# Row sums from a column of ones, two output banks, and one ring of four PSUM banks for every other product

## The reference

```python
# layer 0, attention (8 heads of 64) and top-2 of 8 experts
kv  = concat(layernorm(ctx), layernorm(x) * kv_gate)
sim = (q * 64**-0.5) @ k.T - max;  sim = where(valid, sim, -1e30)
x  += tanh(g) * (softmax(sim) @ v) @ Wout
act = silu(x @ w1.T) * (x @ w3.T);  x += tanh(g) * sum_of_two_experts(act @ w2.T)
# layer 1, attention (16 heads of 64) and a quantised feed-forward with a conv over tokens
x  += tanh(g) * (softmax(q @ k.T / 8 + mask) @ v) @ Wout
h   = silu(conv3(bit_linear(layernorm(x), w1)));  x += tanh(g) * bit_linear(h, w2)
```

## Time and profile before

| | |
|---|---|
| runs | 1537.44, 1544.24, 1548.83 us |
| span of the profiled execution | 1538.1 us, 45142 instructions |
| PE busy | 1278.3 us (83%) |
| POOL busy | 1107.9 us (72%) |
| DVE busy | 1053.8 us (69%) |
| ACT busy | 979.1 us (64%) |
| DMA queues, share of 16 engines | 55.7% on q1, 10.6% on q10 |

### The profile page before, as it was taken

One profiled execution on the slowest core, in us unless ns is written; L12 is line 12 of the kernel. 1 busy time (PEld: TensorE's weight loads), 2 busy tenths in 40 slices (PEclk: granted clock), 3 DMA queues, 4 the chain that ended last, 5 costly groups with the idle time before them and its releaser, 6 DMA issues.

```text
span 1538.1 us, 45142 instructions
## 1 busy us (share of the span) xinstructions
PE 1278.3 (83%) x16918; PEld 994.2 (65%) x16918; DVE 1053.8 (69%) x2830; ACT 979.1 (64%) x2319; POOL 1107.9 (72%) x1359
## 2 busy tenths in 40 slices
PE   0778787679878989878999999899999999998852
PEld 0556565557667866656887887667676676766642
DVE  4768788977556656665666666777777777877634
ACT  2778787456455666554656566678777777777631
POOL 4768788687557755466777776788878888787653
PEclk9989999879999989989999999999999999999965
DMA  9599997486999954368999997344555444555310
GB/s 314 134 193 235 246 239 174 83 221 188 218 233 252 233 95 97 73 159 171 247 258 231 269 247 181 79 97 98 105 91 94 90 105 94 106 82 91 79 32 6
DMA packets 438329, 239.96 MB, mean 156 GB/s; under 512 B 388848, under 2 KB 420320, under 8 KB 429024
## 3 DMA queue, kind: packets, MB, share of 16 engines
q1 hardware_dynamic: 408216, 178.51, 55.7%
q10 hardware_dynamic: 26824, 51.22, 10.6%
q0 software_dynamic: 3072, 7.34, 1.6%
HBM read 107.78 MB, written 35.50 MB: 93 GB/s over the span
## 4 chain that ended last, share of the span: by engine, by line
PE 39%; ACT 13%; DVE 12%; POOL 11%; issue 9%; DMA 9%; DVEq 3%; SPq 2%; ACTq 1%; POOLq 0%
PE bank_ring L1088 9%; PE bank_ring L1126 6%; PE bank_ring L1074 5%; PE bank_out L1107 5%; DVE scores L1340 4%; DMA expert_up<-experts_up 4%; ACT scores L849 4%; PE bank_x L1187 3%; POOL probs L654 3%; PE bank_scores L1048 3%; ACT probs L856 3%; PE bank_x L1140 3%; DMA probs_turned<-probs 3%; ACT values L876 2%; DMA context<-in_ctx 2%
## 5 line engine op out<-in xcount | busy, mean ns | idle before, releaser
L654 POOL TENSOR_TENSOR probs<-scores,probs 112x487 f16<-112x487 f32 x384 | 425.0, 1123 | 234.2 <-ACT probs L856 229.1
L849 ACT ACTIVATE scores<-scores,score_min 112x487 f32<-112x487 f32 x384 | 265.8, 693 | 121.0 <-DVE score_min L1340 118.2
L1357 DVE SCALAR_TENSOR_TENSOR values<-bank_ring,values 128x512 f16<-128x512 f32 x192 | 132.4, 689 | 216.4 <-ACT values L876 216.3
L1340 DVE CUSTOM_DVE_ANT_0 scores<-bank_scores,mask 112x487 f32<-112x487 f32 x384 | 238.1, 657 | 2.9 <-PE bank_scores L1048 2.9
L856 ACT ACTIVATE probs<-scores 112x487 f16<-112x487 f32 x384 | 214.2, 604 | 24.4 <-DMA probs_turned<-probs 9.0
L1088 PE MATMUL bank_ring<-weights,kv_B 128*128 128x128 f16 x3072 | 198.3, 223 | 1.2 <-DVE keys L1352 1.2
L876 ACT ACTIVATE values<-bank_ring 128x512 f16<-128x512 f32 x192 | 112.9, 588 | 128.9 <-PE bank_out L1107 125.2
L1088 PEld LDWEIGHTS bank_ring<-weights,kv_B 128*128 128x128 f16 x3072 | 187.2, 100 | 10.5 <-DVE keys L1352 2.0
L1107 PE MATMUL bank_out<-values,probs_turned 128*128 128x64 f16 x4608 | 171.9, 195 | 17.7 <-issue 11.4
L1074 PE MATMUL bank_ring<-kv_B,weights 128*128 128x488 f16 x768 | 181.0, 372 | 0.0
L1107 PEld LDWEIGHTS bank_out<-values,probs_turned 128*128 128x128 f16 x4608 | 160.1, 100 | 21.4 <-issue 14.0
(11 more groups left out here) (230 smaller groups left out, 2470.9 us busy)
## 6 DMA issues: line engine op xcount, KB each, us to landing
expert_up<-experts_up SPq DMA_DIRECT2D x43, 1024.0 KB, 5.5
expert_down<-experts_down SPq DMA_DIRECT2D x43, 512.0 KB, 6.6
raw_weights<-in_weights ACTq DMA_DIRECT2D x8, 1536.0 KB, 10.7
experts_up<-expert_up ACTq DMA_DIRECT2D x8, 1024.0 KB, 4.4
raw_weights<-in_weights ACTq DMA_DIRECT2D x6, 1024.0 KB, 8.0
probs_turned<-probs SPq DMA_TRANSPOSE x384
context_turned_B<-kv_B ACTq DMA_DIRECT2D x16, 375.0 KB, 8.7
kv_B<-context_turned_B ACTq DMA_DIRECT2D x16, 375.0 KB, 3.7
```

What stands on the lines that cost most here:

```text
L654: pool.tensor_tensor(PR[:, u % 4, 1, 0:KEYS], S[:, u % 4, 0:KEYS], PR[:, u % 4, 0, 0:KEYS], ALU.subtract).then_inc(probs_split, 1)
L849: act_e.activation(S[:, u % 4, 0:KEYS], S[:, u % 4, 0:KEYS], ACT.Exp, bias=rmin[:, u % 4:u % 4 + 1], scale=-1.0, accum_out=rsum[:, g % 2, ...
L1340: dve.tensor_tensor_reduce(out=S[:, u % 4, 0:KEYS], in0=bS[u % 2][0:TOK, 0:KEYS], in1=mask[:, m, 0:KEYS], scale=1.0, scalar=3.0e38, op0=AL ...
L1357: dve.scalar_tensor_tensor(vN[:, j % 2, 1].rearrange("p t d -> p (t d)"), bank("v", j)[:], 1 / WSCALE, vN[:, j % 2, 0].rearrange("p t d -> ...
```

## The change

It does four things.

1. The values get a 65th column per head (`vN` is laid out as 8 blocks of 66 columns): ones in the hi half, zeros in the lo half. So `sum_values` writes the row sum beside the 64 output columns, and the exponentials on ACT no longer accumulate it.
2. There are two output banks. `norm_out` runs twice per group, for four heads each, in step 4g+4 and in step 4g+6 (for two groups 4g+5), and now stands ahead of the reads of `late(j-1)` in DVE's order. `sum_values` waits for the half that was two halves back.
3. ACT rounds the probabilities of both heads in one instruction of 974 elements instead of two of 487.
4. `bank_x0` and `bank_x1` are gone. Queries, `down` and all side products take their place in a common ring of four banks, in PE's order. A product waits until the one four places before it has been read. Two waits that the single bank had implied are now written out (`o_proj` on `o_turn`, `f_up` on `f_turn`).

PE's own order of products stays as it was.

The diff, cut to its core:

```diff
-X0_TASKS = ("m_gate", "route", "wsum")
...
+def side_tasks():
+    tasks = []
     for j in range(FIRST_STEP, LAST_STEP + 1):
...
+        tasks += early(j) + late(j)
+    return tasks
+SIDE_AT = {t: i + 1 for i, t in enumerate(side_tasks())}
...
-RING = 3
+RING = 4
 def ring_uses():
     uses = []
     for j in range(FIRST_STEP, LAST_STEP + 1):
         m = micro(j)
         if is_pair(j + 2):
-            uses.append(("k", j + 2))
+            uses += [("q", j + 2), ("k", j + 2)]
         if m[0]:
             uses.append(m[0])
+        uses += early(j)
         if is_pair(j):
             uses.append(("v", j))
+        if m[1]:
+            uses.append(m[1])
+        uses += late(j)
         if m[2]:
             uses.append(m[2])
...
-        vN = sb("values", [128, 2, 2, 4, 128], F16)
+        vN = sb("values", [128, 2, 2, 8, HW], F16)
...
-        bO, bX0, bX1 = ps("bank_out"), ps("bank_x0"), ps("bank_x1")
+        bO = [ps("bank_out_0"), ps("bank_out_1")]
...
             def split_probs(u):
-                pool.wait_ge(probs_ready, u + 1)
+                pool.wait_ge(probs_ready, u // 2 + 1)
...
             def exp(u):
-                g = u // 8
                 act_e.wait_ge(scores_masked, u + 1)
-                if u % 8 == 0 and g >= 2:
-                    act_e.wait_ge(out_normed, g - 1)
                 act_e.activation(S[:, u % 4, 0:KEYS], S[:, u % 4, 0:KEYS], ACT.Exp,
-                                 bias=rmin[:, u % 4:u % 4 + 1], scale=-1.0,
-                                 accum_out=rsum[:, g % 2, u % 8:u % 8 + 1])
+                                 bias=rmin[:, u % 4:u % 4 + 1], scale=-1.0)
-            def round_probs(u):
+            def round_probs(j):
+                u = 2 * j
                 if u >= 4:
                     act_e.wait_ge(turned[(u - 4) % PT_BUFS], turns_done(u - 4))
+                    act_e.wait_ge(turned[(u - 3) % PT_BUFS], turns_done(u - 3))
-                act_e.activation(PR[:, u % 4, 0, 0:KEYS], S[:, u % 4, 0:KEYS], ACT.Copy).then_inc(probs_ready, 1)
+                act_e.activation(PR[:, u % 4:u % 4 + 2, 0, 0:KEYS], S[:, u % 4:u % 4 + 2, 0:KEYS], ACT.Copy)\
+                    .then_inc(probs_ready, 1)
...
                 last = RING_USES[i]
-                if last[0] == "k":
+                if last[0] == "q":
+                    pe.wait_ge(q_split, last[1] + 1)
+                elif last[0] == "k":
                     pe.wait_ge(k_split, last[1] + 1)
                 elif last[0] == "v":
                     pe.wait_ge(v_split, last[1] + 1)
+                elif last[0] == "up":
+                    pe.wait_ge(gated, 2 * tile(last[1], last[2]) + last[3] + 1)
+                elif last[0] == "down":
+                    pe.wait_ge(down_copied, tile(last[1], last[2]) + 1)
                 else:
-                    pe.wait_ge(gated, 2 * tile(last[1], last[2]) + last[3] + 1)
+                    pe.wait_ge(side_drained, SIDE_AT[last])
...
             def sum_values(j):
                 pe.wait_ge(v_split, j + 1)
+                m = j // 2
+                if j % 2 == 0 and m >= 2:
+                    pe.wait_ge(out_normed, m - 1)
                 for h in range(2):
                     u = 2 * j + h
-                    if u % 8 == 0:
-                        pe.wait_ge(out_normed, u // 8)
...
-                            last = pe.matmul(bO[:, col:col + HD], PT[u % PT_BUFS][:, at:at + 128],
-                                             vN[:, j % 2, b, t, HD * h:HD * h + HD], start=i == 0, stop=i == 11)
+                            last = pe.matmul(bO[m % 2][:, col:col + HD + 1], PT[u % PT_BUFS][:, at:at + 128],
+                                             vN[:, j % 2, b, 2 * t + h, 0:HD + 1], start=i == 0, stop=i == 11)
...
             def down(b, i):
                 t = tile(b, i)
-                pe.wait_ge(x0_drained, X0_AT[("down", b, i)] - 1)
+                ring_free("down", b, i)
+                bD = bank("down", b, i)
...
             def part(task):
                 name, n = task[0], task[1]
-                if name in X0_TASKS:
-                    pe.wait_ge(x0_drained, X0_AT[task] - 1)
-                else:
-                    pe.wait_ge(x1_drained, X1_AT[task] - 1)
+                ring_free(*task)
+                bX = bank(*task)
...
+            for i in range(2):
+                dve.memset(vN[:, i, 0, :, HD:HD + 1], 1.0)
+                dve.memset(vN[:, i, 1, :, HD:HD + 1], 0.0)
...
-            def norm_out(g):
-                dve.wait_ge(values_summed, 8 * g + 8)
-                if g:
-                    dve.wait_ge(x1_filled, X1_AT[("o_turn", g - 1)])
-                dve.reciprocal(rinv[:], rsum[:, g % 2])
+            def norm_out(m):
+                g, half = m // 2, m % 2
+                dve.wait_ge(values_summed, 4 * m + 4)
+                if g and half == 0:
+                    dve.wait_ge(side_filled, SIDE_AT[("o_turn", g - 1)])
+                heads = bO[half][0:TOK, 0:4 * HW].rearrange("p (h d) -> p h d", h=4)
+                r = rinv[:, 4 * half:4 * half + 4].rearrange("p (h o) -> p h o", o=1)
+                dve.reciprocal(r, heads[:, :, HD:HD + 1])
                 dve.drain()
...
+                dve.tensor_tensor(wide[:, 256 * half:256 * half + 256].rearrange("p (h d) -> p h d", h=4),
+                                  heads[:, :, 0:HD], r.to_broadcast([TOK, 4, HD]), ALU.mult).then_inc(out_normed, 1)
...
+                for g in range(PAIRS // 4):
+                    if j == 4 * g + 4:
+                        norm_out(2 * g)
+                    if slack(g) and j == 4 * g + 6:
+                        norm_out(2 * g + 1)
                 for t in late(j - 1):
                     part(t)
-                for g in range(PAIRS // 4):
-                    if slack(g) and j == 4 * g + 6:
-                        norm_out(g)
...
                     if not slack(g) and j == 4 * g + 5:
-                        norm_out(g)
+                        norm_out(2 * g + 1)
```

More of the change, by code:

```diff
@@ L21 @@
 HD = 64
+HW = HD + 2
 EXPERTS, EB = 8, 4
@@ L207, in l1_chunk @@
     return range(j - L1_STEP, j - L1_STEP + 1) if 0 <= j - L1_STEP < L1_CHUNKS else range(0)
-X0_TASKS = ("m_gate", "route", "wsum")
-def ordinals():
-    x0, x1 = [], []
+def side_tasks():
+    tasks = []
     for j in range(FIRST_STEP, LAST_STEP + 1):
-        if is_pair(j + 2):
-            x0.append(("q", j + 2))
-        for t in early(j):
-            (x0 if t[0] in X0_TASKS else x1).append(t)
-        found = micro(j)
-        x0 += [m[:3] for m in found[:2] if m and m[0] == "down"]
-        for t in late(j):
-            (x0 if t[0] in X0_TASKS else x1).append(t)
-    return {t: i + 1 for i, t in enumerate(x0)}, {t: i + 1 for i, t in enumerate(x1)}
-X0_AT, X1_AT = ordinals()
+        tasks += early(j) + late(j)
+    return tasks
+SIDE_AT = {t: i + 1 for i, t in enumerate(side_tasks())}
 def halves_in_step(j):
     return is_pair(j)
-RING = 3
+RING = 4
 def ring_uses():
@@ L509, in load_expert @@
                     if t >= 2:
-                        sp.wait_ge(x0_filled, X0_AT[("down",) + ((b, i - 2) if i >= 2 else (0, TILES[0] - 2 + i))])
+                        sp.wait_ge(down_ready, t - 1)
                     sp.dma_start(edown[:, t % 2], down_dram[e]).then_inc(down_loaded[t % 2], 16)
@@ L514, in store_result @@
                 t = tile(b, i)
-                sp.wait_ge(x0_drained, X0_AT[("down", b, i)])
+                sp.wait_ge(down_copied, t + 1)
                 sp.dma_start(ys[b][128 * i:128 * i + 128, :], yo[:, t % 2]).then_inc(y_stored[t % 2], 16)
@@ L661, in split_hidden @@
                 if t >= 2:
-                    pool.wait_ge(x0_filled, X0_AT[("down",) + ((b, i - 2) if i >= 2 else (0, TILES[0] - 2 + i))])
+                    pool.wait_ge(down_ready, t - 1)
                 pool.wait_ge(gated, h + 1)
@@ L875, in round_v @@
                     act_e.wait_ge(values_summed, 2 * (j - 1))
-                act_e.activation(vN[:, j % 2, 0], bank("v", j)[:].rearrange("p (t d) -> p t d", t=4), ACT.Copy,
+                act_e.activation(vN[:, j % 2, 0, :, 0:HD], bank("v", j)[:].rearrange("p (t d) -> p t d", t=8), ACT.Copy,
                                  scale=1 / WSCALE).then_inc(v_hi, 1)
@@ L888, in copy_result @@
                 t = tile(b, i)
-                act_e.wait_ge(x0_filled, X0_AT[("down", b, i)])
+                act_e.wait_ge(down_ready, t + 1)
                 if t >= 2:
                     act_e.wait_ge(y_stored[t % 2], 16 * (t // 2))
-                act_e.activation(yo[:, t % 2], bX0[:, 0:DIM], ACT.Copy).then_inc(x0_drained, 1)
+                act_e.activation(yo[:, t % 2], bank("down", b, i)[:, 0:DIM], ACT.Copy).then_inc(down_copied, 1)
             def part(task):
@@ L1055, in proj_q @@
                 wq, _, _, step = layer_chunks(j)
-                pe.wait_ge(x0_drained, X0_AT[("q", j)] - 1)
+                ring_free("q", j)
+                bQ = bank("q", j)
                 i = 0
@@ L1060, in proj_q @@
```

(11 more changed lines are left out.)

178 lines of the change are left out of this document (88 added, 90 removed).

## The result

The changed kernel took 1575.33, 1577.46, 1599.03 and 1575.47 us, median 1576.47 of all four; the kernel before 1537.44 to 1549.43 us, median 1546.53 over four runs. The ratio is 1.020, 95% interval 1.016 to 1.024; it leaves out the disturbed 1599.03. The forecast was 1573, range 1541 to 1598, and slower with 0.63. The profiled execution has a span of 1573.6 us, 35.5 more than before.

A forecast was written before the change was run, and what follows sets the result against it. PE was taken as nearly full in both expert stretches, so new waits lengthen the kernel. Terms -5 + 30 - 5 + 27 - 20 - 6 + 6 + 2 = +29 on 1538.1 give 1567, plus 6.1 for the runs: 1573 us, range 1541 to 1598.

The forecast's parts named there:

- The ring in the expert steps: Steps 39 to 55 and 80 to 103: new PE stalls for banks not yet read, 37.6 and 25.0 us.
- The half normalisations' 4.9: Expert stretches: a half normalisation ahead of a late read costs 0.7 us, seven times in either stretch, 4.9 us each.
- What the loads of weights hide: Steps 39 to 55: a later PE waits less for experts' weights, hiding an estimated 8 us of stalls.
- The first rival: Steps 39 to 55: the experts' loads set the pace and stalls only fill waits; 1547 us, chance 0.17.
- The gain in steps 104 to 183: Steps 104 to 183: bank waits of 3.5 us per eight steps go, about 1.5 come new; -20 us.
- Steps 0 to 38: First stretch: removed bank waits mostly turn into the next wait, behind POOL's mask and the router; -5 us.
- The clock: PE: ten new stalls over 2 us, about half followed by the lower clock level; +6 us.
- The third rival: PE: each stall of over 0.8 us, about 39, lowers the clock; 1617 us, chance 0.06.
- The column of ones: PE's sums: 24 more columns for each of 192 pairs at 0.42 ns a column; +2 us.
- The fourth rival: PE's sums: the odd width of 65 columns costs as much as 128; 1640 us, chance 0.02.
- The read-outs on ACT: ACT: 384 row-sum read-outs of 0.19 us disappear, 73 us of busy time; costed at nothing in kernel time.
- The second rival: Softmax on ACT is the path, so shorter exponentials let DVE's key reads come earlier; 1530 us, chance 0.13.

The follow-up runs named there:

- ring of five, keys first: Ring of four banks made five, with one output bank and DVE's keys' lo half moved ahead of the gating; 1514.91 us, ratio 0.982 against the kernel before.
- the ring of four alone: Changed kernel with parts 1 to 3 undone, leaving only the common ring of four banks; 1568.99 us, ratio 1.014 against the kernel before.
- the keys first: Changed kernel with DVE's lo half of the keys moved ahead of the gating and early reads; 1552.10 us, ratio 1.001 against the kernel before.

## Why the prediction was right, and where its terms were off

The mechanism was right: the two expert stretches and the waits in them came as forecast. That the whole span is off by only 6.5 us is in part luck. Steps 0 to 38 and 104 to 183 came out 12 us each above their terms, against 7 in steps 39 to 55 below theirs and the 8 us for clock and column that stood beside the table.

- *The ring in the expert steps, the largest term: right.* The stalls stand where the subtraction of starts and read ends put them, at `down`, the values and the first expert half. 37.6 + 4.9 us were counted in steps 39 to 55 and 38.5 measured; 29.9 and 29.0 in steps 80 to 103. The half normalisations' 4.9 in the first stretch was 3.6, and went into waits for weights. The ring alone has the loss, and either another distance or another order of DVE's reads takes it away.
- *What the loads of weights hide: mis-sized.* I read the 23.0 us of waits for weights as all in steps 39 to 55, and those of 80 to 103 as none; 19.9 stood in the first and 3.1 in the second. I took 8 us; 17.5 of 19.9 went (19.9 to 2.4). 38.5 - 17.5, less the 4.0 of other waits at `down` that the trace of before has there, plus 5.8 more busy us of PE, is 22.8; the stretch grew by 22.6. The first rival had this mechanism, but the stalls outgrew the waits that could hide them. It falls as the whole story: the stretch did not keep its 189 us, and the DMA share fell from 0.96 to 0.82.
- *The gain in steps 104 to 183: the step that failed.* -20 was forecast, -7.6 came. I costed the single rounding at nothing, covered by the sums two steps later. The path is another: through ACT's order to the values' hi half and from there to a bank of the ring; undoing it gave 5.9 us, of which that wait shows 3.1. The waits on single banks went as forecast (all 40.4 us of PE's waits there before are gone), but the new ones came to 27.2 us where I had about 15: 15.4 in place of 11 for values behind late reads, 11.1 in place of 3 behind the keys. PE's busy time is 5.8 us longer, where I had 2 for the column in the whole kernel. Putting the normalisation back behind the reads took 6.9 us off. With both undone the stretch is 18.4 us under the kernel before.
- *Steps 0 to 38: sign not as forecast, cause open.* -5 was forecast, +7.4 and +15.0 came in two profiles of the same kernel. The sums' wait for the transposes was 5.7 us before, and 14.3 and 28.7 after. It does not give the length by itself: the stretch took 294.1 us with 9.0 of that wait (normalisation and roundings undone), 296.2 with 17.9 (ring of five, keys first) and 298.4 with 10.5 (the ring of four alone). What shifts the transposes, and how much of the difference is the change's, stays open; the kernel before has one profile only.
- *The clock: near the forecast in size, and it varies.* In steps 39 to 55 eight products of 12 or 24 matmuls took 1.8 to 2.8 us in place of 1.5, where four did before: 8.3 us of extra time against 4.0, so 4 us for the forecast's 6. The granted clock fell from 0.95 to 0.94. With the row sums on ACT again, and nearly the same stalls, it was 0.98. PE's busy time is not a measure of it: it rose by 5.8 us in that stretch, but also by 4.5 us in steps 80 to 103, where the granted clock stayed at 1.00 with 31 stalls of up to 1.5 us. The third rival falls. The swing that the Trainium skill, "TensorE: Matmul & The Clock Gate", section "A second HAM failure mode: psum-queue depth-cycling", reports of another kernel does not show in those steps.
- *The column of ones: right in size, with a wrong step in its range.* PE's time for the 4608 sums went from 171.9 to 173.1 us in the page's groups; 24 sums take 0.89 us against 0.86. The fourth rival falls. But I misread the layout: the blocks of 65 stand 66 columns apart in the output bank, so each begins at a multiple of 264 bytes, and none in the middle of a line of 8. What the Trainium skill, "PSUM — Partial Sum Buffer", section "Specifications (TRN2)", says of lines of 8 bytes is not tested by this kernel, and was no reason for the far end.
- *The read-outs on ACT: right as a cost of nothing, wrong in the number.* ACT's busy time fell by 48.5 us, not 70 (979.1 to 930.6), and the read-outs are only part of that: with the accumulation back it is 960.7, so they are worth 30.1, since they overlap the exponentials. With two roundings it is 949.6, so the single rounding took off 19.0, which I had not counted. With the accumulation back, the stretches from step 56 on did not change by more than 2.5 us. The second rival falls: PE's stalls behind the keys stayed at 23.4 and 8.0 us then (23.6 and 8.0 in the changed kernel), and moving the read inside DVE's own order removed them, with ACT as it was.

## What to carry to other kernels

When products share a ring, ask for each of them how late its bank's last reader ends against the product's start in the old trace; that subtraction gave the new stalls to within 4 us, and it prices a ring of five as easily as a ring of four. The reader's place in its own engine's order matters as much as the number of banks: two lines moved in DVE's program took back some 24 us. An instruction that is merged with its neighbour inherits the waits of both, and what to look at is what stands behind it in its own queue.

## What the runs showed that was not expected

In steps 104 to 183 of the changed kernel one DVE conversion (112x256, SBUF to SBUF) takes 1.8 to 1.9 us where it took 0.29 before. In nine of sixteen sequences it starts 0.4 to 0.5 us after the beginning of an indirect gather on POOL, and ends 0.16 us after the end of POOL's next tensor operation. Where it starts in the gap between two gathers, or 0.2 to 0.3 us into one (in the ring of four alone and the keys first), it takes 0.29. No run changes the gather or that operation alone, so the cause is not shown. Nothing says that it bounds the stretch: with the keys first four of the nine take 0.29 and the stretch is 471.1 us, and with the normalisation behind the late reads all nine were as long and the stretch was 6.9 us shorter.
